# Channel moments of the next image and the convolution diagonals move from VectorE to ScalarE

## The reference

```
# layer 0: x = x + conv_ref(group_norm(x))
g = v.reshape(B, 32, C // 32, H, W)
m, s = mean(g, (2, 3, 4)), var(g, (2, 3, 4));  xn = (g - m) / sqrt(s + 1e-5)
feat = gelu(dwconv3x3(xn, conv1)); feat = feat * channel_attention(feat)
feat = gelu(dwconv3x3(feat, conv2)); scores -> sort the 4x4 patches
... selective scan over the sorted tokens, unsort ...
# layer 1, on tokens t: t = t + attention(layer_norm(t))
top-2 of 8 experts:  t = t + sum_k p_k * (layer_norm(t) @ expert_w[k] + expert_b[k])
```

## Time and the profile before

| what | value |
|---|---|
| median of 3 runs | 5706.22 us (5703.51 to 5708.03) |
| profiled execution, its own time | 5710.99 us |
| its span, first to last instruction | 5708.9 us |
| busy: VectorE | 4925.1 us, 86% of the span |
| busy: TensorE | 4840.9 us, 85% |
| busy: ScalarE | 3936.4 us, 69% |
| busy: GpSimd | 1610.3 us, 28% |
| mean granted clock of TensorE | 0.943 of full |

### The profile page before, as it was taken

The page is one execution under the profiler, slowest core; times in us unless marked ns, Lnnn a source line. Parts: engine busy times, 40 slices in busy tenths (PEclk is TensorE's granted clock), DMA queues, the critical chain, the costliest instruction groups (busy, mean ns, idle before and its releaser), DMA issues. The chain is left out here.

```text
span 5708.9 us, 100723 instructions
## 1 busy us (share of the span) xinstructions
PE 4840.9 (85%) x34256; PEld 2049.1 (36%) x34328; DVE 4925.1 (86%) x6398; ACT 3936.4 (69%) x5625; POOL 1610.3 (28%) x790
## 2 busy tenths in 40 slices
PE   5788879998788887999878887799986888879997
PEld 2333433333333343333433334333343333433334
DVE  6799679998789967999868996799986899679998
ACT  3777468993477837999347783789924777379992
POOL 1488500000048850000004884000000588400000
PEclk9899989999889998999988999899988899989998
DMA  1000020000000002000000000200000000020000
GB/s 40 0 1 0 15 64 9 9 5 23 23 0 1 0 15 64 9 9 5 23 23 0 1 0 15 64 9 9 5 23 23 1 1 0 15 64 9 9 5 15
DMA packets 41638, 87.27 MB, mean 15 GB/s; under 512 B 11672, under 2 KB 27872, under 8 KB 38112
## 3 DMA queue, kind: packets, MB, share of 16 engines
q1 hardware_dynamic: 41184, 81.11, 5.3%
HBM read 26.55 MB, written 8.39 MB: 6 GB/s over the span
## 5 line engine op out<-in xcount | busy, mean ns | idle before, releaser
L1483 ACT ACTIVATE arena<-ps 128x1024 f32<-128x1024 f32 x2048 | 1913.4, 1033 | 196.9 <-PE ps L1446 183.7
L1512 DVE TENSOR_TENSOR arena<-arena 128x1024 f32<-128x1024 f32 x1664 | 1901.5, 1216 | 35.0 <-ACT arena L1483 34.4
L1122 DVE TENSOR_TENSOR_SCAN arena<-ps,hlast,arena 128x512 f32<-128x512 f32 x1024 | 1251.3, 1265 | 26.5 <-ACT hlast L1007 12.1
L1067 POOL TENSOR_TENSOR arena<-arena 128x1024 f32<-128x1024 f32 x512 | 1200.7, 2355 | 241.0 <-ACT arena L990 173.0
L1446 PE MATMUL ps<-arena 128*32 128x512 f16 x16384 | 1097.4, 384 | 124.7 <-issue 46.7
L1429 PE MATMUL ps<-arena 128*32 128x512 f32 x8192 | 1071.3, 601 | 7.6 <-ACT arena L1483 3.9
L913 PE MATMUL ps<-arena,ident 128*128 128x512 f32 x2048 | 965.4, 595 | 1.1
L1004 ACT ACTIVATE ps<-arena,amat 128x512 f32<-128x512 f32 x1024 | 705.1, 689 | 372.2 <-DVE arena L1122 365.3
L1446 PEld LDWEIGHTS ps<-arena 128*32 128x32 f16 x16384 | 468.3, 98 | 982.1 <-issue 640.9
L1826 POOL MEMSET arena<- 128x1024 f32 x4 | 3.8, 952 | 2646.1 <-POOLq L101 2646.1
L1098 DVE TENSOR_TENSOR arena<-arena,ps 128x1024 f32<-128x1024 f32 x416 | 497.2, 1195 | 86.1 <-remote 62.6
(11 more groups left out here) (257 smaller groups left out, 4578.5 us busy)
## 6 DMA issues: line engine op xcount, KB each, us to landing
arena<-x SPq DMA_DIRECT2D x32, 512.0 KB, 5.2
arena<-arena SPq DMA_DIRECT2D x64, 256.0 KB, 6.0
arena<-arena SPq DMA_DIRECT2D x64, 224.0 KB, 5.8
arena<-arena SPq DMA_DIRECT2D x28, 512.0 KB, 3.5
arena<-pe SPq DMA_DIRECT2D x256, 32.0 KB, 1.8
out<-arena SPq DMA_DIRECT2D x8, 1024.0 KB, 3.9
expw<-L_ffn_expert_w SPq DMA_DIRECT2D x1, 512.0 KB
wqkv<-L_attn_W_qkv SPq DMA_DIRECT2D x1, 192.0 KB
```

Of the source, the lines that this page charges most:

```text
L1067: pool.tensor_tensor(halves(hb[s % RING]), halves(hb[s % RING]), cs[s % 4].unsqueeze(1).broadcast_to([128, HD, CH]), ALU.mult).then_inc(hc ...
L1122: dve.tensor_tensor_scan(halves(hb[s % RING])[:, h, :], da(s, h), halves(injected)[:, h, :], k.hlast[:, s, h, :], ALU.mult, ALU.add).then_ ...
L1483: act.activation(probs[p % 8], k.bank(2 * group[p], 2 * CH), ACT.Exp, scale=SCALE / SPLIT ** 2).then_inc(exp_s, 1)
L1512: dve.tensor_tensor(acc[p % 2], acc[p % 2], probs[p % 8], ALU.add).then_inc(acc_s, 1)
```

## The change

- `setup` and `ffn` get two new pieces of work on ScalarE. `channel_mean` is one pass over the 128x4096 image with `Copy` and an accumulated sum, and two scalings of one column. `channel_variance` is one pass with `Square`, the negated mean as bias and an accumulated sum, and one scaling. The passes write their 4096 columns to a place that nothing reads (`k.at(4096, L)`).
- In `ffn` they treat the next image: the mean ahead of ScalarE's copy of group 3, the variance ahead of that of group 5. In `setup` they treat the first image, behind the wait for its load.
- `score_and_sort` takes `mv` from there. VectorE's eight diagonals, eight `bn_stats` and the `bn_aggr` fall away.
- ScalarE makes the eight diagonals: it first asks for the table of `Sqrt`, makes four of them, takes the root of the group norm, and makes the other four.
- SyncE loads the next image in the last pass of the loop too (image 0 again, because ScalarE's passes run there as well); the result is not used.

```diff
+def channel_mean(k, act, step, loaded, junk):
+    S, x = k.small, k.at(X_AT, L)
+    act.wait_ge(loaded, 64)
+    step(act.activation(junk, x, ACT.Copy, accum_out=S[:, S_MEAN:S_MEAN + 1]))
+    step(act.mul(S[:, S_NMEAN:S_NMEAN + 1], S[:, S_MEAN:S_MEAN + 1], -1.0 / L))
+    step(act.mul(S[:, S_MEAN:S_MEAN + 1], S[:, S_MEAN:S_MEAN + 1], 1.0 / L))
+
+def channel_variance(k, act, step, junk):
+    S, x = k.small, k.at(X_AT, L)
+    step(act.activation(junk, x, ACT.Square, bias=S[:, S_NMEAN:S_NMEAN + 1], accum_out=S[:, S_VAR:S_VAR + 1]))
+    step(act.mul(S[:, S_VAR:S_VAR + 1], S[:, S_VAR:S_VAR + 1], 1.0 / L))
 # setup, ScalarE
+            act.wait_ge(zeroed, 6)
+            moments = Chain(act, k.sem("moments"))
+            channel_mean(k, act, moments, k.sem("x_in"), k.at(4096, L))
+            channel_variance(k, act, moments, k.at(4096, L))
 # score_and_sort, VectorE
-            for n in range(2):
-                for t in range(PT):
-                    dve.tensor_scalar(diag[:, n, t, :], k.ident[:, :], k.convw[:, n, t:t + 1], None, ALU.mult).then_inc(diag_s, 1)
-            for n in range(NCH):
-                step(dve.bn_stats(stats[:, n, :], x[:, n * CH:(n + 1) * CH]))
-            step(dve.bn_aggr(mv, stats))
             step(dve.tensor_copy(g2[:, 0:1], mv[:, 0:1]))
 # score_and_sort, ScalarE
+            k.ready_table(act, ACT.Sqrt, 1)
+            for t in range(PT):
+                act.activation(diag[:, 0, t, :], k.ident[:, :], ACT.Copy, scale=k.convw[:, 0, t:t + 1]).then_inc(diag_s, 1)
             act.wait_ge(gn_var, 1)
             act.activation(rstd, t0, ACT.Sqrt).then_inc(gn_std, 1)
+            for t in range(PT):
+                act.activation(diag[:, 1, t, :], k.ident[:, :], ACT.Copy, scale=k.convw[:, 1, t:t + 1]).then_inc(diag_s, 1)
 # ffn, ScalarE
+            moments = Chain(act, k.sem("moments"))
             for g in range(NG):
+                if g == 3:
+                    channel_mean(k, act, moments, k.sem("x_in"), k.at(4096, L))
+                if g == 5:
+                    channel_variance(k, act, moments, k.at(4096, L))
                 act.wait_ge(fm, g + 1)
 # ffn, SyncE
-            with sp.If(b < B - 1):
-                k.load_x(sp, (b + 1) % B, k.sem("x_in"))
+            k.load_x(sp, (b + 1) % B, k.sem("x_in"))
```

More of the change, by code:

```diff
@@ L138, in patch_tiles @@
     return tiles[:, at:at + n].rearrange("p (x h w) -> p x h w", x=PS, w=W // PS)
+S_MEAN, S_VAR, S_NMEAN = 152, 153, 154
+def channel_mean(k, act, step, loaded, junk):
[8 more added lines that the diff above has]
+    step(act.mul(S[:, S_VAR:S_VAR + 1], S[:, S_VAR:S_VAR + 1], 1.0 / L))
 def setup(k):
@@ L264, in score_and_sort @@
     S = k.small
-    stats = S[:, 0:48].rearrange("p (n s) -> p n s", s=6)
-    mv, g2, gm, rstd, t0, t1 = S[:, 48:50], S[:, 50:52], S[:, 52:53], S[:, 53:54], S[:, 54:55], S[:, 55:56]
+    g2, gm, rstd, t0, t1 = S[:, 50:52], S[:, 52:53], S[:, 53:54], S[:, 54:55], S[:, 55:56]
+    mv = S[:, S_MEAN:S_MEAN + 2]
     csum, ctot, hid, ca = S[:, 56:56 + NG], S[:, 64:65], S[0:C // 4, 65:66], S[:, 66:67]
```

## The result

The changed kernel takes 5675.55 us (median of 6 runs, 5673.23 to 5682.22) against 5707.84 (6 runs, 5703.51 to 5711.89). The ratio is 0.9945, 95% interval 0.9932 to 0.9958: 32.3 us less, where 20.8 less was forecast. 5675.55 also lies just under the stated range, which began at 5677. The forecast of 5685.4 started from a median of 5706.22; from 5707.84 the same sum gives 5687.0. The sign was right, and the amount is more than the chain at the start of an image can give. So the question is where some 11 us come from.

What follows compares the result with a forecast made beforehand. VectorE was taken as the limit at each image's start and in the experts, with no engine setting the pace everywhere. -31.40 + 2.19 + 8.39 = -20.8 us, from 5706.2 to 5685.4 us; range 5677 to 5698.

Steps and rivals of the forecast that it cites:

- The prefix (-31.40): Start of each image: VectorE's diagonals and statistics, 7.80 to 7.92 us an image, leave the path; 31.40 us less.
- the root (+2.19): Start of each image: ScalarE's root comes 0.69 us late in the first, 0.50 in the others; 2.19 us given back.
- The table load: Rival at each image's start: a drain of 1.38 us after ScalarE's table load, 5.5 us in all, 5690.9; 4%.
- The passes in the experts (0): Experts: ScalarE's mean (4.3 us) and variance (4.1 us) fit its 7.55 us idle gaps and cost nothing.
- The rival of a shared SBUF: Experts: ScalarE's passes slow VectorE's additions by reading SBUF at once; at 0.60 us an addition, 5723; 3%.
- The setup (+8.39): Setup: ScalarE's two passes start only when the first image has landed, nothing hides them; 8.39 us added.
- The late instruction fetch: Rival behind the loop's branch: one more stop of 4.0 us in each of three images, 5697.4; 7%.
- From there on the stages only shift: Behind the start of each image, later stages move in time without changing length; 0 us.
- The clock: Rival: the shift redeals TensorE's low-clock stretches; four longest images add 14.2 us (5699.6, 5%), four shortest take 8.9 (5676.5, 4%).

Runs made afterwards that it cites:

- before_d8: The kernel before with 8 one-column VectorE copies added ahead of L331 in each image; +12.8 us against 5707.29 (ratio 1.0021).
- before_d12: The kernel before with 12 one-column VectorE copies added ahead of L331 in each image; -0.9 us against 5707.29 (ratio 0.9999).
- diagonals only: The kernel before with only the eight diagonals moved to ScalarE, VectorE still taking the statistics; 5687.38 us against 5707.04 (ratio 0.9973).

## Why the prediction was wrong

- **The prefix (-31.40) and the root (+2.19).** Right. `sort` lost 30.5 us against 29.2; of this TensorE's first convolution group, for which VectorE waits 2.98 us in the second image and not 3.73, is again the clock. The root was late by 0.35 us in the second image (VectorE waits 0.62 for it, 0.27 before) and by 0.65 in the first; 0.50 and 0.69 were forecast. Four unchained diagonals take 1.26 us, not 1.30.
- **The table load.** It ends at 1449.85 and the activation starts at 1449.86 in the changed kernel, so there is no drain of 1.38 us behind the load to pay, and the rival falls. Nor is there one ahead of a load: the one at 1512.49 in the kernel before follows an activation that ends at 1512.48. The drain that the Trainium skill ("ScalarE: Activation LUTs", What ACT_TABLE_LOAD costs) adds to a load is not in these traces.
- **The passes in the experts (0).** Right: 4.18 us from 1404.68 to 1408.86, 3.65 us of the gap left, no slower additions. The rival of a shared SBUF falls.
- **The setup (+8.39).** Right: first barrier 8.4 us later.
- **The late instruction fetch.** TensorE, ScalarE and VectorE start on time in the changed kernel, no second stop. But `before_d8` shows that the first stop is not a constant: 1.3 us more on VectorE in all three images. No run shows that instruction fetch is behind either.
- **The step that failed** is "From there on the stages only shift". They shift, and by that their low-clock stretches change: 13.3 us less in the profiled launch, and 11.5 and 9.2 us beyond the sum in the two medians. The clock stood among the rivals, as four images like the shortest, 8.9 us and 4%. Its price came from the spread of image lengths inside one launch of the kernel before. These images were no fair draw: project had the same 62.1 us in each, where 60.2 and 58.5 are possible. A spread inside one kernel does not bound what all its images share. Against this rival the prediction held that all four images must fall alike, and for project in the kernel before they had. Nothing in the trace of the kernel before alone said that its deal was a bad one, so the direction could not have been called, and that the surplus was a gain is luck; but the range should have reached well below 5677.

What is shown and what is argued: that project, `ffn` and the output stage of `attention` differ with the granted clock at unchanged instructions is shown, for project down to the single groups of matmuls. That delay alone can do the same is measured in one kernel clear of noise, `before_d12`. That the kernel before lies some 6 us above its relatives rests on eleven medians and fourteen profiles. Why its launches, on several chips, bring the bad deal back stays open: the trace shows no cause that ties the clock's changes to the start of a launch. The Trainium skill ("TensorE: Matmul & The Clock Gate", Part 1) holds that the gate looks at the array on a rhythm of its own, so that cold stretches vary from run to run. Our launches agree in that: one kernel's project took 60.2 us in one launch and 62.0 in another, in three of the changed kernel's four images. That medians some 10 us away from the sum came back is not explained by it.

## What to carry to other kernels

Sum the chain on the path for what an edit does, and read its own stage for whether it did it: in the changed kernel both agreed within 1.5 us, in diagonals only within 3 (`sort` lost 9.5 for 6.5). For the total of a kernel whose TensorE rises from and falls to its lower clock many times, add a deal that all iterations may share; here it was worth -13 to +7 us in 5700, beside 21 us for the edit. To tell the two apart, run the same kernel with several small delays at the place of the edit before believing a surplus or a loss of a few tenths of a per cent. One is not enough: three delays here lay 4.7 us below, 6.7 above and 10.0 below their sums.

## What the runs showed of the hardware that was not expected

- More work can cost nothing: 12 copies of 0.19 us on the path of each image left the median at -0.9 us (interval -5.7 to +4.6, where the sum is +9.1), and 8 cost 12.8.
- One project stage of 100 matmuls takes 61.9 to 62.1, 60.1 to 60.2 or 58.5 to 58.6 us, at a mean granted clock of 0.86, 0.91 or 0.94: steps, with nothing between in the 56 projects profiled. A group of four 512-column matmuls takes 3.78 us at the lower clock and 1.98 at the full one, and stands on one side or the other.
- Launches of one and the same kernel differed by 16.4 us with 8 copies (5708.84 at a mean granted clock of 0.950, 5725.21 at 0.943).
- The stop behind the loop's branch was 8.24 to 8.36 us of idle VectorE in the kernel before and 9.57 to 9.68 in one that differs by eight small instructions, while ScalarE was on time; with 4 and with 12 such instructions it was 8.22 to 8.33.
